# A two-layer graph network: the node rows of the first layer kept in order of places for the first layer norm

## The reference, cut to what matters

```python
def _L0_gnn_ref(x, W, b, gamma, beta, edge_index):
    ...                                   # self loops, norm = dinv[src] * dinv[dst]
    for l in range(W.shape[0]):           # 3 layers, 512 x 512
        h = x @ W[l].T
        agg = jax.ops.segment_sum(h[src] * norm[:, None], dst, num_segments=N) + b[l]
        mean, var = ...                   # over the nodes
        x = jax.nn.relu(gamma[l] * (agg - mean) * jax.lax.rsqrt(var + BN_EPS) + beta[l])
    return x

x = _layernorm(x + _L0_gnn_ref(x, ...), axis=-1)      # the stage around the change
x = _layernorm(x + _L1_gnn_ref(x, ...), axis=-1)
```

## Time and profile before

| | us |
|---|---|
| median of 3 runs (lowest, highest) | 1854.98 (1854.6, 1856.04) |
| the profiled execution's own time | 1854.7 |
| its span, first to last instruction | 1853.0 |

### The profile page before, as it was taken

One profiled execution on the slowest core, in us unless ns is written; L12 is line 12 of the kernel. 1 busy time (PEld: TensorE's weight loads), 2 busy tenths in 40 slices (PEclk: granted clock), 3 DMA queues, 4 the chain that ended last, 5 costly groups with the idle time before them and its releaser, 6 DMA issues. The chain is left out here.

```text
span 1853.0 us, 27588 instructions
## 1 busy us (share of the span) xinstructions
PE 1396.9 (75%) x8180; PEld 1204.7 (65%) x8180; DVE 1206.3 (65%) x3308; ACT 982.5 (53%) x1960; POOL 1048.5 (57%) x1095
## 2 busy tenths in 40 slices
PE   4669599999968999996699999353333239999833
PEld 4558488888856888885588888242232128888722
DVE  6575466666637777763699997464444239999865
ACT  3743144444425777762566664385656634444476
POOL 4773757777534787774423320577777744333236
PEclk8995699999987999998799999566655569999955
DMA  2000556666545766753555552888786532233112
GB/s 58 2 2 1 151 196 222 218 223 220 192 161 205 260 250 241 252 200 143 212 180 220 210 185 107 257 279 271 256 267 234 200 118 84 88 90 91 52 62 112
DMA packets 98920, 313.66 MB, mean 169 GB/s; under 512 B 34576, under 2 KB 36064, under 8 KB 98802
## 3 DMA queue, kind: packets, MB, share of 16 engines
q0 software_dynamic: 62720, 183.99, 29.5%
q1 hardware_dynamic: 36082, 128.24, 19.6%
HBM read 161.18 MB, written 156.39 MB: 171 GB/s over the span
## 5 line engine op out<-in xcount | busy, mean ns | idle before, releaser
L851 PE MATMUL ps_b<-yhi,whi 128*128 128x500 f32 x960 | 390.3, 407 | 8.6 <-DVE ylo L718 8.6
L851 PE MATMUL ps_b<-yhi,wlo 128*128 128x500 f32 x960 | 375.2, 391 | 0.0
L851 PE MATMUL ps_b<-ylo,whi 128*128 128x500 f32 x960 | 374.9, 390 | 0.0
L795 ACT COPY aggT<-ps_b 128x500 f32<-128x500 f32 x240 | 137.9, 574 | 347.1 <-PE ps_b L851 347.1
L747 DVE BATCH_NORM_STATS2 stat<-aggT 128x6 f32<-128x500 f32 x240 | 163.2, 680 | 200.4 <-ACT aggT L795 198.3
L635 POOL DMA_INDIRECT rows<-rows_out,node_at x160 | 187.0, 1169 | 118.3 <-ACT rows_out L800 82.7
L1068 PE MATMUL fin_ps_x<-ident,fin_X 128*127 128x128 f32 (+1 forms) x320 | 75.4, 405 | 176.9 <-DVE fin_xr L1000 163.4
L851 PEld LDWEIGHTS ps_b<-yhi,whi 128*128 128x128 f32 x960 | 182.5, 190 | 40.1 <-DVE ylo L718 9.1
L851 PEld LDWEIGHTS ps_b<-yhi,wlo 128*128 128x128 f32 x960 | 181.4, 189 | 37.8
L851 PEld LDWEIGHTS ps_b<-ylo,whi 128*128 128x128 f32 x960 | 182.4, 190 | 30.8
L1068 PEld LDWEIGHTS fin_ps_x<-ident,fin_X 128*127 128x127 f32 (+1 forms) x320 | 65.8, 298 | 192.8 <-DVE fin_xr L1000 169.2
(11 more groups left out here) (344 smaller groups left out, 3319.8 us busy)
## 6 DMA issues: line engine op xcount, KB each, us to landing
z<-aggT SPq DMA_DIRECT2D x60, 1000.0 KB, 5.3
X<-z SPq DMA_DIRECT2D x40, 1000.0 KB, 5.3
fin_X<-z SPq DMA_DIRECT2D x20, 1000.0 KB, 6.8
rows<-rows_out,node_at POOLq DMA_INDIRECT x160, 3.1
own_row<-in_L_gnn_W SPq DMA_DIRECT2D x2, 1024.0 KB, 10.6
others<-ord_nodeid,ord_place_node POOLq DMA_INDIRECT x80, 2.1
R<-in_x,node_at POOLq DMA_INDIRECT x80, 3.6
G<-rows,srci POOLq DMA_INDIRECT x80, 5.3
```

What stands on the lines that cost most here:

```text
L795: nc.scalar.copy(f.aggT[t % 2][:, j, :], f.ps_b[j % 2][:, 0:COLS]).then_inc(x["copied"], 1)
L851: o = nc.tensor.matmul(f.ps_b[j % 2][:, 0:COLS], w[:, c, j * P:(j + 1) * P], y[b % 2][:, c, :], start=(c == 0 and i == 0), stop=(c == C - ...
```

## The change

In the first layer, SP stores every gathered tile of x a second time, into a new DRAM tensor `x_rows` in the order of places (block, partition, tile, feature), before its z store of the turn. POOL's gather into a tile of `f.R` now also waits until the store from it has landed (`r_out`).

In the first layer norm, POOL gathers nothing: SP loads the four tiles of a block with one plain transfer from `x_rows` (8 KB a partition) into a ring of four blocks, after the z load of the same block. The 16 clearing instructions of POOL go. Of the four scalings of a block into `f.out`, those of the two edge tiles are done by DVE in place of ACT, with a `tensor_scalar` at the end of DVE's turn; POOL waits for the two kinds by a semaphore each.

```diff
@@ layer_stage
+    r_in, r_out = ([m.sem(f"{tag}_{n}{i}") for i in range(8)] for n in ("r_in", "r_out"))
...
+                if first and runs(t + 2):
+                    for j in range(4):
+                        n = 4 * (t + 2) + j
+                        sp.wait_ge(r_in[n % 8], 16 * (n // 8 + 1))
+                        sp.dma_start(x_rows[t + 2, :, j, :], f.R[n % 8][:]).then_inc(r_out[n % 8], 16)
                 if runs(t):
                     sp.wait_ge(x["copied"], C * (t + 1))
                     sp.dma_start(z_out[t], f.aggT[t % 2][:]).then_inc(kept[t % 2], 16)
...
                 ge(pool, x["turned"], n - 7)
+                ge(pool, r_out[n % 8], 16 * (n // 8))
                 pool.indirect_dma_start(f.R[n % 8][:], None, a.x, ...)
@@ finish_gcn
             for b in range(3):
                 sp.dma_start(f.X[b][:], z_in[b]).then_inc(z_got[b], 16)
+                sp.dma_start(f.xr[b][:], x_rows[b]).then_inc(x_in[b], 16)
             prep.load(sp)
             for b in range(3, NB):
                 sp.wait_ge(x["turned"], 4 * (b - 2))
                 sp.dma_start(f.X[b % 3][:], z_in[b]).then_inc(z_got[b % 3], 16)
+                ge(sp, x["normed"], 4 * (b - 3))
+                sp.dma_start(f.xr[b % 4][:], x_rows[b]).then_inc(x_in[b % 4], 16)
...
-                for j in range(4):
-                    if runs(t + 4):
-                        n = 4 * (t + 4) + j
-                        ge(pool, x["normed"], n - 15)
-                        pool.indirect_dma_start(f.xr[n % 16][:], None, a.x, ...)
...
-            for r in range(16):
-                nc.gpsimd.memset(f.xr[r][:], 0.0).then_inc(x["zero"], 1)
-            pool.wait_ge(x["zero"], 16)
...
+                if runs(t):
+                    for j in range(2):
+                        n = 4 * t + j
+                        dve.wait_ge(x["normed"], n + 1)
+                        ge(dve, put[n % 8], 16 * (n // 8))
+                        nc.vector.tensor_scalar(f.out[n % 8][:], f.x2[n % 8][:], f.rstd2[t % 2][:, j:j + 1], None,
+                                                ALU.mult).then_inc(x["edge_out"], 1)
                 prep.vector_late(dve, turn)
...
-                    for j in range(4):
+                    for j in range(2, 4):
                         n = 4 * t + j
                         ge(act, put[n % 8], 16 * (n // 8))
                         act.wait_ge(x["normed"], n + 1)
                         nc.scalar.activation(f.out[n % 8][:], f.x2[n % 8][:], ACT.Copy,
-                                             scale=f.rstd2[q][:, j:j + 1]).then_inc(x["outed"], 1)
+                                             scale=f.rstd2[q][:, j:j + 1]).then_inc(x["plain_out"], 1)
@@ build
+        x_rows = m.dram("x_rows", [m.NB, P, 4, d])
-            f.xr = [m.sb(f"fin_xr{i}", [P, d]) for i in range(16)]
+            f.xr = [m.sb(f"fin_xr{i}", [P, 4, d]) for i in range(4)]
```

More of the change, by code:

```diff
@@ L561, in layer_stage @@
 @stage
-def layer_stage(m, k, f, layer, a, source, table, z_in, z_out):
+def layer_stage(m, k, f, layer, a, source, table, x_rows, z_in, z_out):
     nc, C, D, NB, ET, EPT, COLS = m.nc, m.C, m.D, m.NB, m.ET, m.EPT, m.COLS
@@ L575, in layer_stage @@
     z_got = [m.sem(f"{tag}_z_got{i}") for i in range(3)]
-    r_in = [m.sem(f"{tag}_r_in{i}") for i in range(8)]
+    r_in, r_out = ([m.sem(f"{tag}_{n}{i}") for i in range(8)] for n in ("r_in", "r_out"))
     id_in = [m.sem(f"{tag}_id_in{i}") for i in range(2)]
@@ L608, in _ @@
                 sp.wait_ge(kept[q], 16 * (NB // 2))
+            if first:
+                for r in range(8):
+                    sp.wait_ge(r_out[r], 16 * (NB // 2))
         @block.gpsimd
@@ L901, in finish_gcn @@
 @stage
-def finish_gcn(m, k, f, a, z_in, x2_dram, out_dram, prep):
+def finish_gcn(m, k, f, a, z_in, x_rows, x2_dram, out_dram, prep):
     nc, C, D, NB, L = m.nc, m.C, m.D, m.NB, m.L
     names = ("vec", "var", "root0", "factor", "act_x", "turned", "summed", "moments", "root1", "small", "var2", "root2",
-             "ready", "normed", "outed", "zero")
+             "ready", "normed", "edge_out", "plain_out")
     x = {n: m.sem(f"fin_{n}") for n in names}
     z_got = [m.sem(f"fin_z_got{i}") for i in range(3)]
-    x_in = [m.sem(f"fin_x_in{i}") for i in range(16)]
+    x_in = [m.sem(f"fin_x_in{i}") for i in range(4)]
     put2, put = ([m.sem(f"fin_{n}{i}") for i in range(8)] for n in ("put2_", "put"))
@@ L951, in body @@
                         i, n = m.tile(t, j)[0], 4 * t + j
-                        pool.wait_ge(x["outed"], n + 1)
+                        pool.wait_ge(x["edge_out" if j < 2 else "plain_out"], 2 * t + j % 2 + 1)
                         pool.indirect_dma_start(out_dram, bass.IndirectOffsetOnAxis(ap=k.node_at[:, i:i + 1], axis=0), f.out[n % 8][:], None,
                                                 bounds_check=m.N - 1, oob_is_err=False).then_inc(put[n % 8], 16)
-            for r in range(16):
-                nc.gpsimd.memset(f.xr[r][:], 0.0).then_inc(x["zero"], 1)
-            pool.wait_ge(x["zero"], 16)
             each_turn(body)
@@ L1044, in body @@
                         ge(act, put2[n % 8], 16 * (n // 8))
-                        nc.scalar.activation(f.x2[n % 8][:], f.xr[n % 16][:], ACT.Identity,
+                        nc.scalar.activation(f.x2[n % 8][:], f.xr[t % 4][:, j, :], ACT.Identity,
                                              scale=f.rstd[q][:, j:j + 1], bias=f.nmr[q][:, j:j + 1]).then_inc(x["normed"], 1)
-                    for j in range(4):
+                    for j in range(2, 4):
                         n = 4 * t + j
@@ L1654, in build @@
                             f.raw = m.sb(f"raw{layer}", [P, C, d])
-                        layer_stage(m, k, f, layer, a, source, table[layer % 2], z[(layer + 1) % 2], z[layer % 2])
+                        layer_stage(m, k, f, layer, a, source, table[layer % 2], x_rows, z[(layer + 1) % 2], z[layer % 2])
                         source = table[layer % 2]
@@ L1683, in build @@
             prep.scratch()
-            finish_gcn(m, k, f, a, z[(m.L - 1) % 2], x2_dram, out, prep)
+            finish_gcn(m, k, f, a, z[(m.L - 1) % 2], x_rows, x2_dram, out, prep)
         with ExitStack() as part:
```

12 lines of the change are left out of this document (5 added, 7 removed).

## The result

| | us |
|---|---|
| changed kernel, median of 4 runs (lowest, highest) | 1769.69 (1768.59, 1771.66) |
| kernel before, median of 4 runs | 1854.79 (1854.13, 1856.04) |
| ratio, with its 95% interval | 0.9542 (0.9525 to 0.9558) |
| span of the profiled execution, before and after | 1853.0, 1766.9 |

The forecast was 1789 with a range of 1766 to 1813. It is the time of rival B (1771, chance 0.23): POOL alone stays the bound. Rival A, the forecast itself (0.44), didn't come true.

What follows compares the result with a forecast made beforehand. The prediction took POOL's list to bound the first layer norm. Stage 74 us shorter, with DMA setting 11.0 us for 16 blocks, tail 8 back: 1854.7 - 74 + 8 = 1788.7, plus 0.3, 1789 us; range 1766 to 1813.

Steps and rivals of the forecast that it cites:

- rival B: First layer norm: POOL alone stays the bound, 84 us less, 1771 us; chance 0.23.
- Rival A: First layer norm: DMA beside POOL sets about 11 us a block, 1789 us, own range 1781 to 1797; chance 0.44.
- the signs that it named for itself: Layer norm: POOL waits for ACT or DMA, DMA share 0.95 or more at 360 to 400 GB/s, pitch 11 us, L1155 last.
- What bounds the kernel now: First layer norm before the change: POOL's list of 64 gathers and 160 scatters bounds the stage, 292 us.
- What goes: First layer norm: 64 gathers of 1.31 us, 83.8 us, leave POOL's list; 160 scatters keep 208 us.
- "What is late next", ACT and DVE: Layer norm: ACT at 8.7 and DVE at 9.4 us a block stay under POOL's 10.4; each `tensor_scalar` takes 0.42 us.
- "What is late next", DMA: Layer norm: DMA limits 16 blocks to 11.0 us each, between bounds of 9.7 and 12.2; last four at 10.4.
- The end of the stage: Layer norm's end: without POOL backlog, the tail of exp, log and DVE's last line ends 8 us after POOL's last scatter.
- The start: Layer norm's start: added loads ahead of z of block 3 against gathers and clearings gone; 0, bounds -8 and +8 us.
- The first layer: First layer: four more stores a block raise the DMA share to about 0.81 but cost 0; uncovered, 52 to 102 us.
- A rule against this sum: Layer norm: the port shared by DVE and POOL could add 17 us to POOL's list; a rival, 1797 us, chance 0.08.

Runs made afterwards that it cites:

- dve_only_2: The kernel before with two scalings a block moved from ACT to DVE, gathers kept: 1854.54 us, ratio 1.0003; on the stalling chip, ratio 0.9931.
- pool_fill_2: The changed kernel with two more clearings of a spare tile on POOL in each layer norm block: 1800.63 us, ratio 0.9709.
- half_loads: The changed kernel loading only half of z and of the x rows from block 4 on: 1769.28 us, ratio 0.9542.
- load_no_dve_2: The changed kernel with all four scalings of a block on ACT: 1767.48 us, ratio 0.953; on the stalling chip, ratio 0.9494.
- out_plain: The changed kernel with scaled tiles stored by SP's plain transfers in place of POOL's second four scatters: 1760.29 us, ratio 0.95.
- direct: The changed kernel without x2: ACT writes final rows in one step, only these are scattered, the edge network gathers from them: 1723.65 us, ratio 0.9293.
- start: The changed kernel with edge network loads behind block 3's loads and turn 0's long edge work behind block 0's normalization: 1766.98 us, ratio 0.953.

## Why the range held, and the forecast was 19 us too high

The range held because its lower end, 1766, took in rival B; the time lies 3.7 us above it. The mechanism of the forecast did not come true. Of the signs that it named for itself, the DMA share and rate came (0.95 to 1.01 at 378 to 401 GB/s); the pitch of 11 us, POOL's waits for ACT or DMA and L1155 at the end of the stage did not. What the prediction had right is what bounded the kernel before, what leaves with the gathers, and that the first layer and the start cost nothing.

- **"What bounds the kernel now": right, and shown.** POOL's list bounds the stage, by the count of instructions times duration and 0.30 us. For the kernel before, the gathers took 82.1 us with them, and dve_only_2 shows that less work for ACT alone brings nothing. For the changed kernel pool_fill_2 has the slope (30.9 of 32.2 us), half_loads leaves the DMA engines 2.2 us at most, and load_no_dve_2 excludes ACT.
- **"What goes": right.** 83.8 us forecast, 82.1 measured; the 160 scatters keep 209.8 us, forecast 208.
- **"What is late next", ACT and DVE: right that both stay under POOL.** A `tensor_scalar` takes 0.483 us, not 0.42, within its bounds of 0.29 and 0.69. The 40 are 2.5 us of DVE time more, which no one waits for.
- **"What is late next", DMA: "I take 11.0" is the step that failed.** It was put near two estimates (10.4 by bytes, 11.2 by share), above their middle. The changed kernel has a pace of 10.5, and out_plain, with POOL lightened, 10.6. The estimate by bytes was near; what limits out_plain is open. The one by share took a gather's cost per byte from a stretch of 20 us and let the share end at 1.0 (1.02 MB at 292 GB/s are 3.5 us and not 3.6, a slip without weight); but the share isn't a stock that runs out: it is 0.96 at 357 GB/s in pool_fill_2 and 1.01 at 401 in the changed kernel. This step was worth 16 x (11.0 - 10.4) = 9.6 us. I had set against B that 395 and 426 GB/s stood for 5 to 10 us only; they hold, at 393 to 412, through five windows of 30 us.
- **"The end of the stage": failed with it.** The tail was to come out by 8 us, because DMA would leave POOL no backlog. POOL kept one, and DVE's last line ended 3.4 us before the last scatter. Where POOL is not the bound the mechanism is there: DVE ends 11.7 us after POOL in out_plain, 9.5 in direct. So it was right as a mechanism and hung on the wrong pace.
- **"The start": right, 0.** The two effects are in the trace: z of block 3 issued 5.7 us later, waited for 5.85 instead of 0.76 us, and the gathers and clearings gone. The first normalization is 0.4 us earlier, though the stage's first load is issued 0.9 us later (1167.37 against 1166.45). That the effects cancel so well is in part luck: the bounds were -8 and +8.
- **"The first layer": right, 0.** PE stays full, the share is 0.82 (forecast 0.81), POOL waits for a store once, for the 0.3 us of its usual pause, and what lies ahead of the layer norm became 0.9 us longer.
- **"A rule against this sum": there, and a tenth of its size.** The Trainium skill, "SBUF — State Buffer", section "SBUF: two separate sides", makes the shared port an exclusive lock for the whole instruction, against a DVE operation in a two-port mode. A full block would have been 19 us in dve_only_2, where the ratio is 1.0003 and the scatters keep their median of 0.972 us. In the changed kernel it is 0.21 us for each of eight scatters. In which mode the `tensor_scalar` ran no trace shows. The scatters beside DVE's L1165, which reads two tiles of SBUF, stretch to 1.64 and 1.09 us again.
- **Not in the prediction: 3.4 us** from the gap between the last scatter and the next stage (11.6 to 8.2 us). It is 11.6 in dve_only_2 too, which still gathers, and 8.2 in load_no_dve_2, 8.5 in pool_fill_2. It isn't the landing of the last scatters: in both traces no byte moves in its last 5 us. What does it was not tried and stays open.

The sum that would have been right is the prediction's own with POOL's pace kept and the tail hidden: 1854.7 - 82.1 - 0.4 = 1772.2; the gap's 3.4 us give 1768.8, against 1768.59 for the profiled execution. From the forecast's side: 9.6 for the pace, 8 for the tail and 3.4 for the gap are 21.0, less 1.8 because the scatters took 209.8 and not 208. The 19.2 that are left are the 19 us.

## What to carry to other kernels

For an engine that works through a list, take the number of its instructions times the duration and the pause between two; what left the list here left the kernel one for one, until a second limit was met. A second limit that comes out about as large as the first is not to be added to it: here two within 0.4 us a block (8 x 1.28 = 10.2 for POOL's list, 10.6 in out_plain) left a pace of 10.5, and the price of the second showed only when the first was cut (out_plain and direct). And a DMA share near 1.0 doesn't show that the DMA engines are the bound: halve the bytes, or pad the other engine, and see which one moves the time.

## What the runs showed of the hardware that was not expected

- One core moved 401 GB/s over 150 us, loads and scatters of 2 KB rows mixed, at a share of 1.01. The Trainium skill, "DMA: Bandwidth & Descriptors", section "Specifications", gives 435 GB/s as the ceiling of the fabric; the trace agrees in so far as it stays below, with 422 GB/s over the ten microseconds from 1170.
- The landing time of a scatter to `out` was 8.3 us in the changed kernel and 3.8 in half_loads, with the same time of the kernel: two blocks of buffers stand behind it.
- The plain load of `l_nexti`, in small pieces, occupies SP's queue for 16.8 us (12.3 in start, 9.7 in the kernel before) and POOL for 2.01. While such pieces move, the DMA engines' share is 1.28 at 120 GB/s.
- A scatter's issue on POOL stretches beside DVE: from 0.97 to 1.18 us beside a `tensor_scalar` of 128x512, eight times in the changed kernel.
- One chip ran the same kernel before in 2069 us and the other in 1854, with engines idle for up to 29.5 us in the layer norm without a wait of the kernel to show for it. load_no_dve gave 5.1% there and 4.7% here, dve_only 0.7% there and nothing here.
